# A macaron block on one core: a batch's turn pieces, the last batch's rank and lookup, the pair loads and the combines put in other slots

## The reference

```python
def _L0_attn_ref(x, Wq, Wk, Wv, fc_w, fc_b):
    Q = einsum('bne,hde->hbnd', x, Wq)              # K, V alike; 3 heads
    scores = einsum('hbnd,hbmd->hbnm', Q, K) / 16
    w = softmax(scores, axis=2)                     # over the queries n
    attn = einsum('hbnm,hbmd->hbnd', w, V)
    return mean(attn, axis=0) @ fc_w.T + fc_b

def _L0_ffn_ref(x, ...):
    scores = sigmoid(x @ gate_w)
    _, selected = top_k(scores + expert_bias[None, :], 2)
    top = take_along_axis(scores, selected, axis=1)
    top = top / (top.sum(-1, keepdims=True) + 1e-20)
    shared = silu(x @ shared_gate_w) * (x @ shared_up_w) @ shared_down_w
    routed = sum over the 16 experts e of
             comb[:, e:e+1] * (silu(g) * u @ experts_down[e]),  g, u = split(x @ experts_gate_up[e])
    return shared + routed

x = x + 0.5 * _L0_ffn_ref(_layernorm(x), ...)
x = x + _L0_attn_ref(_layernorm(x), ...)
x = x + 0.5 * _L0_ffn_ref(_layernorm(x), ...)
```

## Time and profile before

| what | value |
|---|---|
| time, median of 3 runs | 512.28 us (509.96 to 513.18) |
| the profiled execution: time, span of its trace | 512.53 us, 511.3 us |
| mean granted clock of TensorE | 0.956 |
| TensorE matmuls (PE) busy | 442.7 us, 87% |
| TensorE weight loads (PEld) | 394.0 us, 77% |
| VectorE (DVE) busy | 342.4 us, 67% |
| ScalarE (ACT) busy | 265.7 us, 52% |
| GpSimd (POOL) busy | 278.3 us, 54% |

### The profile page before, as it was taken

The page is one execution under the profiler, slowest core; times in us unless marked ns, Lnnn a source line. Parts: engine busy times, 40 slices in busy tenths (PEclk is TensorE's granted clock), DMA queues, the critical chain, the costliest instruction groups (busy, mean ns, idle before and its releaser), DMA issues. The chain is left out here.

```text
span 511.3 us, 10128 instructions
## 1 busy us (share of the span) xinstructions
PE 442.7 (87%) x2951; PEld 394.0 (77%) x2951; DVE 342.4 (67%) x1053; ACT 265.7 (52%) x708; POOL 278.3 (54%) x322
## 2 busy tenths in 40 slices
PE   1676799999787899999999999989979888999982
PEld 1345699899666789988889888979868677899972
DVE  6589575565448575458646875675685786777778
ACT  4855376676523455543544454435434663577750
POOL 5267875565064643386344746738657167266660
PEclk9977699999989999999999999999998988999995
DMA  8672375576632100011000111104001466366968
GB/s 295 242 226 92 114 210 160 189 207 130 160 94 63 53 21 1 1 52 35 28 12 22 53 31 50 57 3 141 31 33 62 153 222 213 102 189 188 303 227 254
DMA packets 44468, 60.33 MB, mean 118 GB/s; under 512 B 6080, under 2 KB 36800, under 8 KB 44416
## 3 DMA queue, kind: packets, MB, share of 16 engines
q1 hardware_dynamic: 34688, 37.11, 23.2%
q0 software_dynamic: 7584, 20.98, 13.7%
q10 hardware_dynamic: 2144, 1.60, 1.0%
HBM read 34.75 MB, written 24.91 MB: 117 GB/s over the span
## 5 line engine op out<-in xcount | busy, mean ns | idle before, releaser
L2099 POOL TENSOR_TENSOR e_sp<-raw,e_sp 128x512 fp32r<-128x512 f32 x48 | 62.2, 1296 | 69.5 <-ACT e_sp L1163 69.0
L400 PE MATMUL bank<-v_sp,e_sp 128*128 128x256 f32 x576 | 78.1, 286 | 2.4 <-DVE x_sb L1703 2.0
L400 PEld LDWEIGHTS bank<-v_sp,e_sp 128*128 128x128 f32 x576 | 75.4, 193 | 6.2 <-issue 2.8
L400 PE MATMUL bank<-g_sp,xT 128*128 128x512 f32 x288 | 75.5, 398 | 0.1
L2063 POOL DMA_INDIRECT raw<-xn_dram,gather_at x47 | 45.6, 971 | 30.9 <-PE bank L406 27.1
L2025 POOL DMA_INDIRECT pair_dram<-raw,slot_i x47 | 45.8, 974 | 30.1 <-ACT raw L1055 26.7
L1186 ACT ACTIVATE raw<-bank,softmax_row 128x512 f32<-128x512 f32 x48 | 33.2, 691 | 55.1 <-DVE softmax_row L1854 54.7
L400 PEld LDWEIGHTS bank<-g_sp,xT 128*128 128x128 f32 x288 | 52.0, 190 | 9.5 <-issue 0.2
L400 PE MATMUL bank<-w_hi,e_sp 128*128 x188 | 51.6, 297 | 1.2 <-DVE e_sp L1672 1.1
L1854 DVE TENSOR_REDUCE softmax_row<-bank 128x1 f32<-128x512 f32 x48 | 32.9, 686 | 25.8 <-PE bank L400 25.3
L1672 DVE TENSOR_TENSOR e_sp<-bank,e_sp 128x128 fp32r<-128x128 f32 x94 | 27.2, 290 | 31.8 <-ACT e_sp L1025 31.1
(11 more groups left out here) (287 smaller groups left out, 1089.6 us busy)
## 6 DMA issues: line engine op xcount, KB each, us to landing
stage<-slab_dram SPq DMA_DIRECT2D x47, 136.0 KB
y_dram<-stage SPq DMA_DIRECT2D x47, 128.0 KB, 3.0
late_pair<-pair_dram SPq DMA_DIRECT2D x16, 256.0 KB, 4.3
slab_dram<-stage SPq DMA_DIRECT2D x17, 136.0 KB
stage<-in_w_pack SPq DMA_DIRECT2D x6, 384.0 KB, 4.9
stage_more<-in_w_pack SPq DMA_DIRECT2D x6, 384.0 KB, 3.2
x_sb<-in_x SPq DMA_DIRECT2D x4, 512.0 KB, 7.0
xn_dram<-xn_all SPq DMA_DIRECT2D x4, 512.0 KB, 5.2
```

The source lines that it names most:

```text
L400: m = pe.matmul(dst, lhs[k][l], rhs[k][r], start=(first and k == 0 and i == 0), stop=(last and k == n - 1 and i == 2), skip_group_check=True)
L2099: pool.tensor_tensor(e_sp[:, i, 1, :], e32[:, i, :], e_sp[:, i, 0, :].bitcast(F32), ALU.subtract).then_inc(s_e_lo, 1)
```

## The change

Five things are put elsewhere; what is computed stays the same, and so do the number and the size of the loads, of the stores and of the combines.

1. **Pair loads.** SP issues the loads of token tiles 0 to 3 behind row loads 34 to 37 (before 37 to 40) and those of 4 to 7 behind 40 to 43 (before 43 to 46).
2. **Combines.** VectorE makes one combine in each of the tile steps 37, 39, 41, 43, 45 and 47, and two in each of the steps 48, 49 and 50. Behind the last step come four more of tiles 4 to 7, two of tiles 8 and 9, then `shared_mul`, one, `shared_lo`, five, the sinks, and eight.
3. **Stores.** Token tiles 0 to 3 are stored from SP's queue, ahead of the load of pair 12, and not from ScalarE's.
4. **A batch's second unit.** In units 13, 25 and 37 (`turn_of_batch`) VectorE's side piece stands behind the values' low half, so `attn_out` comes sooner.
5. **The last batch's list.** TensorE's `rank_again` and `pack_table` move one slot later, VectorE's `write_table` behind the next piece of the list, and one memset to another batch.

```diff
-    PAIRS_AT = {37: 0, 38: 1, 39: 2, 40: 3, 43: 4, 44: 5, 45: 6, 46: 7}
+    COMBINES_AT = {37: 1, 39: 1, 41: 1, 43: 1, 45: 1, 47: 1, 48: 2, 49: 2, 50: 2}
+    PAIRS_AT = {34: 0, 35: 1, 36: 2, 37: 3, 40: 4, 41: 5, 42: 6, 43: 7}
...
                 yield from prev_front(b - 1)
-                for _ in range(2 if b < B - 1 else 3):
+                for _ in range(2 if b < B - 1 else 4):
                     yield
                 rank_again(b - 1)
                 yield
                 if b == B - 1:
-                    for _ in range(4):
+                    for _ in range(5):
                         yield
                     pack_table(False)
...
-            for q in range(LATE_T):
+            for q in range(TB, LATE_T):
                 act.wait_ge(s_comb, combined(q))
                 act.dma_start(out_rows[q], x_sb[:, q, :]).then_inc(s_out, 16)
...
                         dve.scalar_tensor_tensor(out=x_sb[:, t, :], in0=late_pair[:, t, k, :],
                                                  scalar=weight[:, k, t:t + 1], in1=x_sb[:, t, :], op0=ALU.mult,
                                                  op1=ALU.add).then_inc(s_comb, 1)
+                        yield
...
                 count_class(b - 1)
+                if b == 1:
+                    chained(dve.memset(full_cap[:], float(FULL_TILES * P)))
                 yield
                 if b == B - 1:
-                    chained(dve.memset(full_cap[:], float(FULL_TILES * P)))
...
                     rest = list_rest()
                     next(rest)
                     yield
+                    next(rest)
+                    yield
                     write_table(False)
-                    next(rest)
-                    yield
                     next(rest)
                     yield
...
-                if b + 1 < B:
+                turn_of_batch = b > 0 and u % PER_BATCH == 1
+                if b + 1 < B and not turn_of_batch:
                     side_pieces(u, b, attn_side, ffn_side)
                 if late is not None:
                     attn_out(late)
-                if b + 1 == B:
+                if b + 1 == B and not turn_of_batch:
                     side_pieces(u, b, attn_side, ffn_side)
                 slab_side(u, b, 0)
...
+                if turn_of_batch:
+                    side_pieces(u, b, attn_side, ffn_side)
                 side_pieces_late(u, b, ffn_side)
                 slab_side(u, b, 1)
...
+            combines = (step for t in range(0, 2 * TB, 2) for step in combine_two(t))
+
             def open_late(s):
                 if s == FULL_TILES:
                     shared_sink(1, 2, (0,))
+                for _ in range(COMBINES_AT.get(s, 0)):
+                    next(combines)
...
             ffn(1, open_late, FULL_TILES, mid=open_mid)
-            for t in range(0, TB, 2):
-                combine_two(t)
+            run(combines)
+            late_combines = (step for t in range(2 * TB, LATE_T, 2) for step in combine_two(t))
+            for _ in range(2):
+                next(late_combines)
             shared_mul(1, 3)
-            for t in range(TB, 2 * TB, 2):
-                combine_two(t)
+            next(late_combines)
             shared_lo(1, 3)
-            for t in range(2 * TB, LATE_T, 2):
-                combine_two(t)
+            run(late_combines)
             shared_sink(1, 3)
             for t in range(LATE_T, NT, 2):
-                combine_two(t)
+                run(combine_two(t))
...
-            for t in range(len(PAIRS_AT), NT):
+            for t in range(len(PAIRS_AT), LATE_T):
+                load_pair(t)
+            for t in range(TB):
+                store(t)
+            for t in range(LATE_T, NT):
                 load_pair(t)
             run(tail2())
```

8 lines of the change are left out of this document (5 added, 3 removed).

## The result

The changed kernel took 515.86 us (median of 14 runs, 512.19 to 517.69), the kernel before 512.22 in the same runs; the ratio is 1.0067, with a 95% interval of 1.0044 to 1.0091. So it is some 3.4 us slower where 1.8 us less was forecast. The profiled execution took 515.81 us, its span 514.6.

A forecast was written before the change was run, and what follows sets the result against it. TensorE was taken to bound attention, with few gaps waiting for VectorE, and VectorE alone the tail. Tail -2.6 + 0.3 + 0.2 and attention -0.2 + 1.75 - 1.25 gave -1.8 us: 510.5 us median, 8-in-10 range 506.0 to 513.2.

The forecast's parts named there:

- tail: Behind the last FFN tile: fewer combines left on VectorE end the chain sooner, 2.6 us gained, ends 0 and 3.6.
- combines in the steps: Last layer's tile steps: moved combines overfill VectorE's idle and delay TensorE, 0.3 us lost, between 0 and 0.9.
- pair loads: SP's queue: earlier pair loads wait for scatters and delay row loads 41 to 43; 0.2 us lost, range 0 to 2.7.
- units 13 and 25: Attention: TensorE's wait before the mix goes as attn_out comes sooner; 0.2 us gained in all, ends 0 and 1.9.
- unit 37: Attention: V's low half no longer hides rstd, so TensorE idles; 1.75 us lost, between a 1.4 gain and 2.6 loss.
- the list: Attention, last batch: TensorE's waits for the choice and tile list partly go; 1.25 us gained, ends 0 and 3.6.
- Rival (2): Last layer: late scatter landing makes row loads late, clock falls there and behind unit 37; 3.1 us slower, 515.4; chance 0.10.
- near 0: Units 13 and 25: size of the two terms under the VectorE and GpSimd contention rule; without it 0.5 us each.
- Whether the clock falls: Unit 37: TensorE's 2.3 us idle may drop its clock, costing 1.6 us; undecided, so half, 0.8, was taken.
- rival (3): Tail bound by the last pair rows, gaining 1.6 us instead of 2.6; 511.5 us; chance 0.70 together with the forecast.
- the 0.3 us taken off for the rows' landing: Tail: last pair rows land at 505.2, just when their first combine is due; cuts the gain from 2.9 to 2.6 us.

The follow-up runs named there:

- tail_only: The kernel before with only the moved combines (with the new order behind the steps) and the four stores on SP; ratio 0.9961, 509.38 us beside 510.94.
- rows_back: The changed kernel with the pair loads back behind row loads 37 to 40 and 43 to 46; ratio to the kernel before 1.0036.
- pairs_only: The kernel before with only the eight pair loads moved three tiles sooner; ratio 1.0030.
- turn_back: The changed kernel with VectorE's side piece of units 13, 25 and 37 in its old place; ratio to the kernel before 0.9999.
- turn_two: The changed kernel with unit 37's side piece in its old place, those of units 13 and 25 still moved; ratio to the kernel before 0.9985.
- list_back: The changed kernel with the last batch's list edits undone; ratio to the kernel before 1.0075.
- list_tail: The kernel before with the moved combines, stores and last batch's list, without moved pair loads or side pieces; ratios 0.9970 and, run again, 0.9960.
- stores_held: The kernel of list_tail with ScalarE's stores of token tiles 8 to 11 held until the third of the last four pair loads landed; ratio 0.9969.
- mix_first: The kernel before with attn_out ahead of the side piece, both still ahead of the values' low half; ratio 1.0073.
- turn_gap: The kernel before with the side piece of units 13 and 25 behind the row_max of the next unit; ratio 1.0023.

## Why the prediction was wrong

1.8 us less was forecast and some 3.4 more measured. By its own steps, in us of the profiled execution (plus is slower):

| step | predicted | in the change | what the runs showed |
|---|---|---|---|
| tail | -2.6 | -0.95 | -1.16 in tail_only, -0.8 to -2.1 in the others |
| combines in the steps | +0.3 | | +0.19 in tail_only, +0.22 in rows_back |
| pair loads | +0.2 | +3.0 | +2.15 in pairs_only, +0.9 in turn_back |
| units 13 and 25 | -0.2 | +1.28 | +1.29 in turn_two |
| unit 37 | +1.75 | +0.85 | +2.40 with the clock's fall (list_back) |
| the list | -1.25 | -0.24 | -1.2 to -1.3 in turn_back and list_tail |

**Pair loads: the step that failed most.** "I take 0.2". The wait ahead of row load 41 was seen, and its bound of 2.7 us was nearly right (3.0 measured); but the landing was taken from rows before the first pair load, and the real one took some 4.9 us, like the earlier trace rows. And the first four loads were priced at nothing: that a row load among three pair loads takes 5.8 us was not in the sum, though the pair load's own 4.3 us was. Rival (2) named this mechanism. That its 515.4 us lies near the measured time is luck in part: it counted 2.4 us for falls of the clock, which the change's trace doesn't have, and nothing at tile 37 or for units 13 and 25. By the ratios the places cost 0.3%, some 1.5 us (the change against rows_back, pairs_only against before), less than the 2 to 3 us of the traces; turn_back, with the same places, lost 1.07 us in its trace, 0.2 of it for the combines. How late a row comes depends on how the steps fall against the landings.

**Units 13 and 25: the right fact on the wrong side.** The text had the hold of VectorE beside GpSimd from the earlier trace rows and let it cancel a gain. It is a cost: 0.96 us on the engine that was found to be the bound, against 0.54 of idle. The rule of the Trainium skill ("SBUF — State Buffer", "Who interferes with whom") that the text weighed, that a VectorE instruction with two SBUF inputs contends with a GpSimd instruction that reads SBUF, is borne out, with 2.02 and 2.58 us for a pair of 1.06 in these traces. But "near 0" isn't what it gives here. The text took the wait of 0.54 as a limit for the gain; it also meant that VectorE has hardly any time to give, so whatever lengthens it is lost.

**Unit 37** went by the steps: `rstd` at 343.92 (343.85 forecast), the transpose at 345.47 (345.6), TensorE's idle 2.27 (2.3), 0.85 us lost (0.95). The times can be set side by side because unit 36 comes at the same time in both traces, which is chance (1.33 us sooner from the start, 1.36 lost on the way). Whether the clock falls was left at a half, and it fell in one trace with this idle (list_back) and not in two others (the change, rows_back). The step lacked what a shift of VectorE does later: some 1.2 us in units 41 to 43, which turn_two and turn_back show by its absence.

**The list** was right in size when nothing else moves: 1.2 to 1.3 us for 1.25, of which some 1.05 had come by unit 43 (0.95 forecast). **The tail** was over-sized: the ends were 0 and 3.6, rival (3) gave 1.6 for a tail bound by the last pair rows, and the traces have 0.8 to 2.1, the change 0.95. The step that was mis-sized is the 0.3 us taken off for the rows' landing: VectorE stood 2.05 us for them in the change, and 0.9 to 1.9 in the other traces with the new tail, stores_held left out. The sum had the scatter's issue and landing as before; in the change that issue was 0.8 us longer.

The 0.37 us between unit 47 and tile 32 belong to no step, and no run explains them; other kernels with two falls of the clock there lie between -0.4 and +0.1 on the first chip.

## What to carry to other kernels

A wait of one engine is a gain only if the engine it waits for can give the time: where VectorE is the bound, moving its pieces to end TensorE's wait moved the wait, and a piece put beside GpSimd's elementwise work took twice its time. In an in-order DMA queue a load that waits for something holds every load behind it, and a deeper ring for those loads didn't help here; before a big load is moved ahead of small ones, price both the wait at its head and the small ones' way among the big. And a shift of one microsecond early on can cost or give another where two engines' work meets later, so a change is worth testing part by part: three of this one's five parts together gain 0.3 to 0.4%, the other two cost some 1%. And two traces are no experiment where traces of one kernel differ: the end behind the last scatter was 12.7 and 13.9 us in two traces of the same program.

## What the runs showed of the hardware that was not expected

- TensorE's granted clock fell to 0.53 and 0.59 in the stretch behind idles of 2.27 us (list_back) and 2.15 us (mix_first), and stayed at 1.00 behind an idle of 2.27 us in the change and 2.28 us in rows_back, at the same place of the program.
- The hold beside GpSimd reaches small instructions and those with one tensor input: `route` of 128x64 took 1.04 us in the change and 1.24 in rows_back, 0.20 to 0.46 in the others. The normalising of a tile took 2.04 us for 0.41 (1.92 already in the kernel before), but it began beside GpSimd's indirect DMA, ahead of the subtraction, so which of the two held it isn't shown. A `row_max`, which reads PSUM, kept its 0.68 us with the subtraction running throughout (turn_gap, 224.75 us), and a pair beside GpSimd's indirect DMA alone kept its 1.06.
- It was VectorE that was held even where its instruction began first by the records: the second of a pair 0.42 us ahead of the subtraction took 2.00 us (mix_first), 0.22 us ahead 1.81 us (turn_gap), for 0.48 alone. GpSimd's subtraction kept its 1.29 us in both.
- TensorE's idle of 2.69 us for the tile list is followed by a fall of the clock in some traces and not in others, and the marks from unit 41 to 47 agree to 0.07 us either way: with VectorE the bound, the lower clock cost nothing there.
- The same program ran 4% longer on two other chips (533 us for 511). By the traces some 17 us of it lie in the last layer and some 5 us ahead of unit 12; the attention from unit 12 to 41 agreed with the first chip's within 0.15 us. Which of the engines or queues is slower there is open.
